# A state-space mixing head: the D factors move from VectorE to GpSimd, and half of a product the other way

## The reference

```python
dt = exp(log_dt)                              # [256]
w = -exp(log_w_real) + 1j * w_imag            # [256, 64]
dtA = w * dt[:, None]
Cm = (C[..., 0] + 1j * C[..., 1]) * (exp(dtA) - 1.0) / w
h = 2 * real(einsum('chn,hnl->chl', Cm, exp(dtA[:, :, None] * arange(512))))
h = h + attention(layernorm(h))               # 16 query heads, 4 key heads of 128, window 256
h = h + gated_low_rank_ffn(layernorm(h))
```

## Time and profile before

| | |
|---|---|
| median of 3 runs | 835.1 us (834.56 to 835.16) |
| profiled execution | 833.84 us, span in the trace 832.0 us |
| busy: PE / DVE / ACT / POOL | 753.5 / 577.2 / 454.5 / 444.6 us |
| mean granted TensorE clock | 0.97 of full |
| head, 0 to 43 us | PE useful work none; POOL idle to 31.66 us |

### The profile page before, as it was taken

The page is one execution under the profiler, slowest core; times in us unless marked ns, Lnnn a source line. Parts: engine busy times, 40 slices in busy tenths (PEclk is TensorE's granted clock), DMA queues, the critical chain, the costliest instruction groups (busy, mean ns, idle before and its releaser), DMA issues.

```text
span 832.0 us, 19710 instructions
## 1 busy us (share of the span) xinstructions
PE 753.5 (91%) x6958; PEld 685.6 (82%) x6958; DVE 577.2 (69%) x1626; ACT 454.5 (55%) x1246; POOL 444.6 (53%) x662
## 2 busy tenths in 40 slices
PE   0277877899999999999999999999999999999985
PEld 0176667899999999999999999999999989899762
DVE  7999648677766666656565566655655687777877
ACT  6644327555555656555575665555656554564420
POOL 0497826544444747444465654444747556555522
PEclk9998989899999999999999999999999999999995
DMA  9033450100010102000001020000100000000002
GB/s 208 0 67 63 86 218 27 39 1 0 0 39 2 52 1 77 0 0 0 0 8 45 10 68 0 0 0 0 52 2 1 1 2 26 25 25 25 1 25 77
DMA packets 30504, 26.48 MB, mean 32 GB/s; under 512 B 22446, under 2 KB 22830, under 8 KB 30198
## 3 DMA queue, kind: packets, MB, share of 16 engines
q1 hardware_dynamic: 30310, 25.77, 10.9%
q10 hardware_dynamic: 144, 0.07, 0.0%
HBM read 17.44 MB, written 8.39 MB: 31 GB/s over the span
## 4 chain that ended last, share of the span: by engine, by line
PE 77%; DVE 11%; POOL 5%; issue 3%; ACT 2%; DMA 1%; DVEq 0%; SPq 0%; POOLq 0%; ACTq 0%
PE bank_quad L1218 17%; PE bank_quad L1220 17%; PE bank_quad L1219 16%; PE bank_pair L1220 4%; PE bank_pair L1218 4%; PE bank_pair L1219 4%; POOL w_lo L423 2%; PE bank_pair L1361 2%; PE bank_pair L1371 1%; PE bank L1371 1%; PE bank L1375 1%; DVE bank_pair L905 1%; PE bank_quad L1314 1%; PE bank_quad L1230 1%; POOL kq_lo L493 1%
## 5 line engine op out<-in xcount | busy, mean ns | idle before, releaser
L1218 PE MATMUL bank_quad<-xt_hi,w_hi 128*128 (+1 forms) x768 | 217.2, 283 | 0.8 <-POOL w_lo L423 0.8
L1220 PE MATMUL bank_quad<-xt_lo,w_hi 128*128 (+1 forms) x768 | 214.9, 280 | 0.0
L1219 PE MATMUL bank_quad<-xt_hi,w_lo 128*128 (+1 forms) x768 | 214.8, 280 | 0.0
L987 DVE TENSOR_TENSOR kq<-bank_quad,cst 128x512 f32<-128x512 f32 (+1 forms) x96 | 57.9, 603 | 140.8 <-ACT swap L679 106.6
L489 POOL TENSOR_TENSOR swap<-swap,cst 128x512 f32<-128x512 f32 (+1 forms) x96 | 105.8, 1104 | 82.3 <-ACT swap L679 79.5
L1218 PEld LDWEIGHTS bank_quad<-xt_hi,w_hi 128*128 128x128 f32 x768 | 144.9, 189 | 2.8 <-POOL w_lo L423 1.4
L1220 PEld LDWEIGHTS bank_quad<-xt_lo,w_hi 128*128 128x128 f32 x768 | 144.7, 188 | 0.0
L1219 PEld LDWEIGHTS bank_quad<-xt_hi,w_lo 128*128 128x128 f32 x768 | 144.6, 188 | 0.0
L351 POOL TENSOR_TENSOR spare<-cst 1x1 f32<-1x1 f32 x87 | 16.6, 191 | 223.3 <-DVE rinv L1121 141.1
L719 ACT ACTIVATE sm<-sm,mx 128x128 f32<-128x128 f32 (+1 forms) x256 | 114.2, 447 | 21.5 <-DVE mx L1111 21.5
L678 ACT ACTIVATE swap<-bank_quad 64x512 f32<-64x512 f32 (+1 forms) x96 | 50.4, 524 | 125.1 <-PE bank_quad L1220 122.6
(11 more groups left out here) (265 smaller groups left out, 1883.2 us busy)
## 6 DMA issues: line engine op xcount, KB each, us to landing
mixed<-st SPq DMA_DIRECT2D x32, 128.0 KB, 2.0
out<-x SPq DMA_DIRECT2D x16, 256.0 KB, 2.0
raw<-in_w_qkv SPq DMA_DIRECT2D x8, 384.0 KB, 3.5
raw<-in_w_o SPq DMA_DIRECT2D x10, 256.0 KB, 2.7
x<-mixed SPq DMA_DIRECT2D x2, 1280.0 KB, 11.0
norm_mem<-in_w_qkv SPq DMA_DIRECT2D x6, 384.0 KB, 3.6
x<-mixed SPq DMA_DIRECT2D x3, 512.0 KB, 4.6
norm_mem<-in_w_o SPq DMA_DIRECT2D x6, 256.0 KB, 2.7
```

Source lines behind the costliest of these rows:

```text
L987: v.tensor_tensor(view(kq), src, table(cosT), ALU.mult).then_inc(kq_cos, 1)
L1218: mmul(dst, lh, rh, start=start and k == 0, stop=False, skip_group_check=True)
L1219: mmul(dst, ll, rh, start=False, stop=False, skip_group_check=True)
L1220: last = mmul(dst, lh, rl, start=False, stop=stop and k == n - 1, skip_group_check=True)
```

## The change

GpSimd starts as soon as `rho` is there (`CH_RHO`) and computes |w|^2 / 2, the polynomial and the whole chain of the D factors, in 42 instructions of its own on 128x128: VectorE's fused forms (`scalar_tensor_tensor`) become two GpSimd instructions each. 25 are `tensor_tensor`, 17 are `tensor_scalar`. A `link` of GpSimd's own (semaphore `pool_chain`) follows 28 of them. VectorE keeps the reciprocal (between `nrm_sum` and `nrm_done`). VectorE takes over the first half of P's magnitudes; GpSimd keeps the second half. The product of v with its magnitudes is now made before that of u, and `d_poles` is signalled by GpSimd's last instruction and waited for by VectorE ahead of the copies into PSUM. `keep_warm(5)` on TensorE now waits for the first `pa_done`, not for `v_done`.

```diff
+            def link(ins):
+                links[0] += 1
+                ins.then_inc(pool_chain, 1)
+                pool.wait_ge(pool_chain, links[0])
-            pool.wait_ge(d_poles, 1)
+            mw = ex[:, 1, :]
+            pool.wait_ge(chain, CH_RHO)
+            pool.wait_ge(wim_in, 16)
+            gp.tensor_tensor(nrm[:], mw, mw, ALU.mult)
+            link(gp.tensor_tensor(wsq[:], wim[:], wim[:], ALU.mult))
+            link(gp.tensor_tensor(nrm[:], nrm[:], wsq[:], ALU.add))
+            gp.tensor_scalar(nrm[:], nrm[:], 0.5, 1.0, ALU.mult, ALU.mult).then_inc(nrm_sum, 1)
+            k, r, q, p2 = (t[:].rearrange("p a b -> p (a b)")[:, 0:P] for t in (kk, rr, qq, ki))
+            link(gp.tensor_scalar(t0[:], rho[:], -87.0, 88.0, ALU.max, ALU.min))
+            link(gp.tensor_scalar(k, t0[:], 1.4426950408889634, ROUND, ALU.mult, ALU.add))
+            link(gp.tensor_scalar(k, k, ROUND, 1.0, ALU.subtract, ALU.mult))
+            link(gp.tensor_scalar(r, k, -0.693359375, 1.0, ALU.mult, ALU.mult))
+            gp.tensor_scalar(p2, k, 127.0, 8388608.0, ALU.add, ALU.mult)
+            gp.tensor_scalar(t1[:], k, 2.12194440e-4, 1.0, ALU.mult, ALU.mult)
+            link(gp.tensor_tensor(r, r, t0[:], ALU.add))
+            link(gp.tensor_tensor(r, r, t1[:], ALU.add))
+            link(gp.tensor_scalar(q, r, 1.0 / 5040, 1.0 / 720, ALU.mult, ALU.add))
+            for c in (1.0 / 120, 1.0 / 24, 1.0 / 6, 0.5, 1.0):
+                link(gp.tensor_tensor(q, q, r, ALU.mult))
+                link(gp.tensor_scalar(q, q, c, 1.0, ALU.add, ALU.mult))
+            link(gp.tensor_tensor(q, q, r, ALU.mult))
...
+            pool.wait_ge(trig_ready, 2)
+            link(gp.tensor_tensor(t1[:], half[:], half[:], ALU.mult))
...
+            pool.wait_ge(nrm_done, 1)
+            link(gp.tensor_tensor(dr, dr, nrm[:], ALU.mult))
+            gp.tensor_tensor(ndi, ndi, nrm[:], ALU.mult)
+            gp.tensor_scalar(ndr, dr, -1.0, 1.0, ALU.mult, ALU.mult).then_inc(d_poles, 1)
...
             pool.wait_ge(trig_ready, 4)
-            for k in range(2):
...
-                nc.gpsimd.tensor_tensor(ptab[:, qs], ptab[:, qs], m, ALU.mult).then_inc(p_mag, 1)
+            gp.tensor_tensor(ptab[:, HALF_Q:NQ], ptab[:, HALF_Q:NQ], half_of_mag(1), ALU.mult).then_inc(p_mag, 1)
...
-            v.tensor_copy(t0[:], rho[:])
-            v.tensor_tensor(nrm[:], mw, mw, ALU.mult)
...
-            q, p2 = expm1_parts(t0[:], P)
...
+            dve.wait_ge(nrm_sum, 1)
+            v.reciprocal(nrm[:], nrm[:]).then_inc(nrm_done, 1)
...
             dve.wait_ge(mag_ready, 3)
+            dve.wait_ge(trig_ready, 1)
+            v.tensor_tensor(vtab[:], v_trig, magnitudes(0), ALU.mult).then_inc(v_done, 1)
             dve.wait_ge(trig_ready, 3)
-            times_mag(utab, 1).then_inc(u_done, 1)
-            link(v.tensor_tensor(t1[:], half[:], half[:], ALU.mult))
...
-            link(v.tensor_tensor(dr, dr, nrm[:], ALU.mult))
-            v.tensor_copy(d_first, dd[:, :, 0:HALF_Q * QH8]).then_inc(d_poles, 1)
+            v.tensor_tensor(utab[:], utab[:], magnitudes(1), ALU.mult).then_inc(u_done, 1)
+            dve.wait_ge(trig_ready, 4)
+            first = slice(0, HALF_Q)
+            link(v.tensor_tensor(ptab[:, first], ptab[:, first], magnitudes(2, first), ALU.mult))
+            dve.wait_ge(d_poles, 1)
+            v.tensor_copy(d_first, dd[:, :, 0:HALF_Q * QH8])
             link(v.tensor_copy(d_rest, dd[:, 0:2, HALF_Q * QH8:]))
...
-            v.tensor_tensor(vtab[:], v_trig, m, ALU.mult).then_inc(v_done, 1)
...
-            pe.wait_ge(v_done, 1)
+            pe.wait_ge(pa_done, 1)
             keep_warm(5)
```

More of the change, by code:

```diff
@@ L315, in tower @@
         w_hi, w_lo, w_lo_dve = sem("w_hi_done"), sem("w_lo_done"), sem("w_lo_dve_done")
-        chain = sem("dve_chain")
+        chain, pool_chain, nrm_sum, nrm_done = sem("dve_chain"), sem("pool_chain"), sem("nrm_sum"), sem("nrm_done")
         mag_ready, ang_ready, trig_ready = sem("mag_ready"), sem("angles_ready"), sem("trig_ready")
@@ L437, in chunk @@
                     ALU.mult).then_inc(g2_ready, 1)
-            pool.wait_ge(d_poles, 1)
-            pool.wait_ge(trig_ready, 4)
-            for k in range(2):
-                qs = slice(k * HALF_Q, (k + 1) * HALF_Q)
-                m = mag[:, 2].rearrange("p (q h) e -> p q (h e)", q=NQ)[:, qs].unsqueeze(2).to_broadcast(
-                    [P, HALF_Q, 2, 64])
-                nc.gpsimd.tensor_tensor(ptab[:, qs], ptab[:, qs], m, ALU.mult).then_inc(p_mag, 1)
+            gp = nc.gpsimd
+            links = [0]
@@ new lines, in _ @@
+            p2 = p2.bitcast(F32)
+            gp.tensor_scalar(t2[:], p2, -1.0, 1.0, ALU.add, ALU.mult)
+            link(gp.tensor_tensor(em1[:], q, p2, ALU.mult))
+            link(gp.tensor_tensor(em1[:], t2[:], em1[:], ALU.add))
+            gp.tensor_scalar(t0[:], em1[:], 1.0, 1.0, ALU.add, ALU.mult)
+            pool.wait_ge(trig_ready, 2)
+            link(gp.tensor_tensor(t1[:], half[:], half[:], ALU.mult))
+            gp.tensor_scalar(t1[:], t1[:], -2.0, 1.0, ALU.mult, ALU.mult)
+            gp.tensor_tensor(ai[:], t0[:], sin1[:], ALU.mult)
@@ new lines, in _ @@
+            link(gp.tensor_tensor(ar[:], em1[:], cos1[:], ALU.mult))
+            link(gp.tensor_tensor(ar[:], t1[:], ar[:], ALU.add))
+            gp.tensor_tensor(dr, ai[:], wim[:], ALU.mult)
+            gp.tensor_tensor(t1[:], ar[:], mw, ALU.mult)
+            gp.tensor_tensor(ndi, ai[:], mw, ALU.mult)
+            link(gp.tensor_tensor(t2[:], ar[:], wim[:], ALU.mult))
+            gp.tensor_tensor(dr, dr, t1[:], ALU.subtract)
+            link(gp.tensor_tensor(ndi, ndi, t2[:], ALU.add))
+            pool.wait_ge(nrm_done, 1)
@@ new lines, in _, with half_of_mag @@
+            link(gp.tensor_tensor(dr, dr, nrm[:], ALU.mult))
+            gp.tensor_tensor(ndi, ndi, nrm[:], ALU.mult)
+            gp.tensor_scalar(ndr, dr, -1.0, 1.0, ALU.mult, ALU.mult).then_inc(d_poles, 1)
+            def half_of_mag(k):
+                return mag[:, 2].rearrange("p (q h) e -> p q (h e)", q=NQ)[:, k * HALF_Q:(k + 1) * HALF_Q].unsqueeze(
+                    2).to_broadcast([P, HALF_Q, 2, 64])
+            pool.wait_ge(trig_ready, 4)
+            gp.tensor_tensor(ptab[:, HALF_Q:NQ], ptab[:, HALF_Q:NQ], half_of_mag(1), ALU.mult).then_inc(p_mag, 1)
@@ L452, in _ @@
             grid = lambda t: t.rearrange("p q (h e) -> p q h e", h=QH8)
-            pool.wait_ge(p_mag, 2)
+            pool.wait_ge(p_mag, 1)
             nc.gpsimd.tensor_tensor(grid(pq[2][:]), grid(ptab[:, second, 0, :]), per_pole(dr), ALU.mult)
@@ L832, in _ @@
                 reduce_angles(k, ang[:, max(k - 1, 0)])
-            v.tensor_copy(t0[:], rho[:])
-            v.tensor_tensor(nrm[:], mw, mw, ALU.mult)
[L835 to L838, removed]
-            q, p2 = expm1_parts(t0[:], P)
-            link(v.tensor_tensor(em1[:], q, p2, ALU.mult))
@@ L841, in _, with magnitudes @@
[L841 to L845, removed]
+            dve.wait_ge(nrm_sum, 1)
+            v.reciprocal(nrm[:], nrm[:]).then_inc(nrm_done, 1)
+            def magnitudes(k, qs=slice(0, NQ)):
+                return mag[:, k].rearrange("p (q h) e -> p q (h e)", q=NQ)[:, qs].unsqueeze(2).to_broadcast(
+                    [P, qs.stop - qs.start, 2, 64])
@@ L847, in _ @@
             dve.wait_ge(mag_ready, 3)
+            dve.wait_ge(trig_ready, 1)
+            v.tensor_tensor(vtab[:], v_trig, magnitudes(0), ALU.mult).then_inc(v_done, 1)
             dve.wait_ge(trig_ready, 3)
-            times_mag(utab, 1).then_inc(u_done, 1)
-            link(v.tensor_tensor(t1[:], half[:], half[:], ALU.mult))
-            v.scalar_tensor_tensor(ai[:], em1[:], 1.0, sin1[:], ALU.add, ALU.mult)
-            link(v.tensor_tensor(ar[:], em1[:], cos1[:], ALU.mult))
-            link(v.scalar_tensor_tensor(ar[:], t1[:], -2.0, ar[:], ALU.mult, ALU.add))
@@ L863, in _ @@
-            v.tensor_copy(d_first, dd[:, :, 0:HALF_Q * QH8]).then_inc(d_poles, 1)
+            v.tensor_tensor(utab[:], utab[:], magnitudes(1), ALU.mult).then_inc(u_done, 1)
[4 more added lines that the diff above has]
+            v.tensor_copy(d_first, dd[:, :, 0:HALF_Q * QH8])
             link(v.tensor_copy(d_rest, dd[:, 0:2, HALF_Q * QH8:]))
-            m = mag[:, 0].rearrange("p (q h) e -> p q (h e)", q=NQ).unsqueeze(2).to_broadcast([P, NQ, 2, 64])
@@ L879, in p_times_d @@
                 v.tensor_tensor(pa[:, qs, r, :], other, pq[r][:], ALU.add).then_inc(pa_done, 1)
-            dve.wait_ge(p_mag, 1)
             p_times_d(0, 0, d_first[:, 2], d_first[:, 0])
@@ L926, in _ @@
                     dve.wait_ge(b_ready, 2 * TURN_AT)
-                    dve.wait_ge(p_mag, 2)
+                    dve.wait_ge(p_mag, 1)
                     p_times_d(1, 1, d_rest[:, 0], d_rest[:, 1])
```

## The result

| | median of 7 | profiled execution | span |
|---|---|---|---|
| before | 834.56 us (833.77 to 835.16) | 833.84 | 832.0 |
| changed | 838.92 us (836.78 to 840.52) | 838.87 | 836.7 |

The ratio is 1.0054, with a 95% interval of 1.0041 to 1.0068: 0.5% slower. 838.1 was predicted, in a range of 834 to 842. That forecast was 3.0 us on top of a median of 835.1; the difference measured is 4.4 us.

What follows compares the result with a forecast made beforehand. The first chunk's start, waiting on GpSimd and VectorE in the head, was taken as the bound: 37.3 - 33.85 - 0.5 = +3.0 us, on 833.8 gives 836.8, with 1.3 more for the median 838.1 us; range 834 to 842.

Steps and rivals of the forecast that it cites:

- The bound and the point of no change: In the head, the first chunk's start sets the time; it moves by D - 33.85 us, with no change at 33.85.
- D: Time of GpSimd's last instruction of the chain of D factors in the head; forecast at 37.3 us.
- The contention: In the head, VectorE instructions reading two SBUF tensors and GpSimd's wait for each other; D at 37.3, alone 29.6 us.
- The nearest-row prices: GpSimd instructions on 128x128, priced from similar trace rows: `tensor_tensor` 0.45 us, `tensor_scalar` 0.33, gap after a `link` 0.08.
- The low end of D: GpSimd's chain counted with the low ends of the instruction prices: D at 35.5 us.
- rival B: Cheap GpSimd instructions and a full TensorE clock: D = 35.5, time 835.5 to 836 us; chance 0.10.
- The holds by u and by half of P: VectorE's u product holds GpSimd's chain off for 1.9 us, its half of P for 0.9.
- The fillers: TensorE's filler matmuls ahead of the first chunk take 5.94 us and cost nothing, by 0.3 us of cover.
- What gives some back: Fillers end 0.3 us before the first chunk; if TensorE's clock stays full there, 0.5 us is won back.
- rival C: Another half-clock stretch in the dense attention costs 1.7 us, two 3.4; 841.5 us with D = 38; chance 0.09, shared.
- Rival A: In the head, VectorE and GpSimd pass each other: D at 29.6 to 30, time 831.4 us; chance 0.11.

Runs made afterwards that it cites:

- experiment 1: Changed kernel with rounded angles in PSUM, so that VectorE's angle passes read only one tensor from SBUF; ratio to the kernel before 1.0011 (0.9999 to 1.0024).
- experiment 3: Changed kernel with VectorE's products of u and of P's first half with their magnitudes left out; ratio to the kernel before 1.0012 (0.9998 to 1.0027).
- experiment 4: Changed kernel with rounded angles in PSUM and VectorE's products of u and P's first half left out; ratio to the kernel before 0.9982 (0.9971 to 0.9993).
- experiment 5: Changed kernel with TensorE's fillers waiting for v's product again, not the first part of P times D; ratio to the kernel before 1.0057 (1.0038 to 1.0077).
- experiment 6: Kernel before, with only P's first half of magnitudes moved to VectorE, behind v's product; ratio to the kernel before 1.0018 (1.0007 to 1.0029).
- experiment 2: Kernel before, with rounded angles in PSUM; ratio to the unedited kernel before 1.0014 (0.9998 to 1.0030).
- experiment 7: Changed kernel with rounded angles in PSUM, GpSimd doing only |w|^2/2 and the polynomial, VectorE the chain of D; 831.25 us, ratio to the kernel before 0.9974.

## Why the prediction was right, and where it wasn't

**The bound and the point of no change: right.** No change was put at D = 33.85. Through all kernels with the whole chain on GpSimd the first chunk's release kept its distance: L489 ends at 37.58 and L433 at 46.65, 9.07 later, and it is 9.07, 9.07, 9.07 and 9.06 in experiments 1, 3, 4 and 5; 9.0 was laid out (D + 6.0 + 3.0). P times D took 4.07 and ended at 42.34, D + 4.76 against D + 4.73.

**The contention: right in mechanism and in sum.** D came at 37.58 against 37.3. Its terms were each a little off and cancelled. The nearest-row prices: `tensor_tensor` 0.46 (0.45 taken), `tensor_scalar` 0.30 (0.33 taken, the low end), gap 0.08. Ten instructions were to be done at the end of the angles, at 19.9; the angles ended at 19.23, and it was eight, the last at 19.39. I had the two engines take strict turns, each making the other wait. VectorE did wait a little (0.08 to 0.14 us) in L867, L880 and the first L874; its other five ran at their old 0.69 and 1.23. L456 waited through both L875 (14.03 to 15.26) and L874 (to 15.98); behind that each of VectorE's held off one GpSimd instruction. So VectorE lost 0.4 us, not 1.1, and GpSimd more than forecast. No run shows the start of 0.19 us of its own that this count gave VectorE; what the runs show of its share is those waits of 0.08 to 0.14. The reciprocal and v's product held nothing off, as forecast: beside them (19.27 to 20.22 and 21.51 to 23.80) GpSimd's instructions took 0.30 and 0.45 to 0.46. The low end of D was summed wrongly too: by its own count it is 35.9, not 35.5, and rival B's time 0.4 later; and the 0.27 us for 256 elements comes to 0.29 by the row it names. D came near neither end. That the one that comes second waits for the whole instruction of the other was read from three places of the trace before; the changed kernel has it again, with 2.22 us for an instruction of 0.30 that waited for L895. What makes it wait isn't shown.

**The holds by u and by half of P: right.** 1.9 and 0.9 were forecast; L467 lost 1.92 and L470 1.01, and experiment 3 gave 3.03 back.

**The fillers: wrong in size.** "The fillers cost nothing, by 0.3 us of cover" took their 5.94 us as fixed. They took 6.77 and held the chunk by 0.34. The ten records are of two kinds, slow and fast. By form, TensorE of the changed kernel from 40.3 to 45.4 and from 45.6 to 47.05, and of the kernel before from 34 to 37 (a record that reaches over an edge counts on both sides):

```profile
L1278 PE MATMUL bank_quad<-cst 128*128 128x512 f32 x7 | 5.5, 955 | 40.4 <-DVE pa L914 40.4
...
L1278 PE MATMUL bank_quad<-cst 128*128 128x512 f32 x4 | 1.9, 592 | 0.0
```

```profile
L1244 PE MATMUL bank_quad<-cst 128*128 128x512 f32 x4 | 3.4, 998 | 34.2 <-DVE vtab L866 34.2
```

The slow ones fill some 5 us in the changed kernel and 3 before. What sets their number isn't shown, and it isn't the time at which they start: in experiment 4 they start at 34.22, before at 34.24, and the ten take 7.20 and 5.94. Over all profiles here they take 5.94 to 7.39.

**What gives some back: right for four chunks, wrong for the head.** Before, TensorE had idled 2.76 us ahead of the first chunk and the clock from 43.90 to 47.30 read 0.50; the 0.5 us that I took off for a clock that stays full was my estimate. It did stay full (1.00 from 47.1 to 49.5), and gave 0.86 at the first chunk (2.09 instead of 2.95) and 0.46 at the third and fourth (3.38 late instead of 3.84). Then TensorE's longer pause in the fourth (0.88 instead of 0.44) took it away, and by the last chunk the delay is 3.88. Such pauses, of 0.2 to 1.2 us, stand in the chunks of the other profiles too, so that it is the change's doing isn't shown. Nor is it shown that the fillers' place kept the clock full: in experiment 6 it was full (1.00) behind 2.59 us of idle time.

**The rest of the kernel: not forecast.** From the last chunk's 3.88 the delay grew to the span's 4.7. The stretches with a low clock in the attention's start, first of the changed kernel, then of the kernel before (columns as in the earlier trace rows):

```profile
130.80:137.60 6.80, 5.10 (x26) 4.93 (x26) 5.91 (x29) 4.97 (x16) 2.89 (x5) 0.54 0.00 0
```

```profile
129.30:132.70 3.40, 3.40 (x18) 3.40 (x18) 2.99 (x22) 2.27 (x10) 2.21 (x4) 0.51 0.01 2
```

The same place of the work has twice the low clock in the changed kernel. I had this as rival C with 1.7 us for one more such stretch; 0.8 was the growth of the whole rest, 0.3 of it between 439 and 457 us, where one matmul stands at 439.39 before and 443.95 now, and a later one at 457.35 and 462.25. It isn't shown to be the change's doing: in experiment 6 the profiled execution's rest was faster than before's, its span 831.2, while its median was slower. I take it for the spread of single executions and don't count it as explained.

So of the 4.4 us between the medians the head has 3.9; 3.0 were forecast. The 0.9 between are 0.3 for D, 0.1 for the way from D to the chunk and 0.5 for the give-back that wasn't kept; the fillers' 0.34 vanished in the second chunk's wait for GpSimd. The forecast of 838.1 lies nearer to 838.92 than 3.0 to 4.4, which is luck: it was built on a median of 835.1, and the kernel before came in at 834.56. Rival A fell with the first row of GpSimd over 1 us; B's cheap `tensor_scalar` was real, its clock gain wasn't kept.

## What to carry to other kernels

An engine that is idle in the profile isn't free for work that a busy neighbour can hold off (6.2 of 26.4 us here): look up which of VectorE's instructions read two tensors from SBUF, and price GpSimd's work beside them by rows in which the two met. With the neighbour's second operand in PSUM the hold went here (GpSimd's L457 from 1.19 to 0.30 us in experiment 1), though the neighbour's own instruction became slower (L874 from 0.69 to 1.23); that pays as long as the neighbour has slack (without it, in experiment 2, the first chunk came 1.75 us later). And move the part that has slack on both sides (here the polynomial, needed at 24.8), not the tail that another engine stands and waits for.

## What was not expected of the hardware

- GpSimd and VectorE don't always take turns one by one. VectorE's L875 and L874, 0.03 us apart, both went by while GpSimd's L456 waited (1.89 us instead of 0.65). The next three held off one GpSimd instruction each; what decides isn't shown.
- GpSimd's L456 (max, min) and L458 (subtract, multiply) took 0.65 and 0.66 us with nothing holding them off, in experiments 1, 4 and 7, where all other `tensor_scalar` of 128x128 took 0.30, the int32 form too. Whether that is the operations or their first use, the runs don't tell.
- TensorE's filler matmuls ran at half pace (0.85 us from start to start instead of 0.43) for the first 3 to 6 us (3.2 before, 4.9 in the changed kernel, 5.9 in experiment 2), although the granted clock reads 1.00 there (40.4 to 45.5 us in the changed kernel). The profile doesn't show why.
- After 16.67 us without a matmul the clock of the stretch from 40.0 to 46.6 us read 0.50, and so did that of the first chunk's stretch, 46.6 to 49.2 (experiment 5).
